# The expert stage of a decoder kernel: gate and up products side by side, and hidden rows turned in their own step

## The reference, cut to what matters

```python
logits = SOFTCAP * jnp.tanh((x @ w_gate) / SOFTCAP)
probs = jax.nn.softmax(logits, axis=-1)
_, idx = jax.lax.top_k(probs, TOPK)
weights = probs * jax.nn.one_hot(idx, E, dtype=probs.dtype).sum(-2)
for e in range(E):
    h = jax.nn.silu(x @ w1[e]) * (x @ w3[e])
    out = out + h @ w2[e] * weights[:, e:e + 1]
```

## Time and profile before

| | |
|---|---|
| time, median of 3 runs | 765.69 us (765.66 to 766.63) |
| profiled execution, its own time | 770.09 us |
| its span, first to last instruction | 767.6 us |
| granted TensorE clock, mean | 0.942 |
| busy in the span: PE, PEld, DVE, ACT, POOL | 654.6, 531.9, 483.6, 436.3, 201.2 us |
| expert stage, first gate product to the last result | about 614 to 742 us |

### The profile page before, as it was taken

The page is one execution under the profiler, slowest core; times in us unless marked ns, Lnnn a source line. Parts: engine busy times, 40 slices in busy tenths (PEclk is TensorE's granted clock), DMA queues, the critical chain, the costliest instruction groups (busy, mean ns, idle before and its releaser), DMA issues.

```text
span 767.6 us, 13772 instructions
## 1 busy us (share of the span) xinstructions
PE 654.6 (85%) x4748; PEld 531.9 (69%) x4749; DVE 483.6 (63%) x1091; ACT 436.3 (57%) x1123; POOL 201.2 (26%) x364
## 2 busy tenths in 40 slices
PE   6788787998999998878978999999986299999950
PEld 4566577998988988843545677777776178778840
DVE  1577776577586577475845656566557567777735
ACT  3988846457456456446866646464523256566622
POOL 2455510040010010011213334252326402223224
PEclk9999999999999999987999999999999589999985
DMA  8995000220220220043020000000078211111114
GB/s 303 378 321 165 1 1 1 86 87 1 88 86 1 86 87 1 1 194 81 1 83 1 1 1 3 1 1 2 1 304 327 68 30 48 48 55 48 48 46 145
DMA packets 31921, 62.02 MB, mean 81 GB/s; under 512 B 2452, under 2 KB 26776, under 8 KB 29624
## 3 DMA queue, kind: packets, MB, share of 16 engines
q1 hardware_dynamic: 29848, 56.04, 21.7%
q0 software_dynamic: 2016, 5.22, 1.9%
HBM read 45.80 MB, written 15.55 MB: 80 GB/s over the span
## 4 chain that ended last, share of the span: by engine, by line
PE 57%; ACT 19%; DVE 15%; issue 4%; POOL 3%; DMA 2%; SPq 0%; POOLq 0%; ACTq 0%; DVEq 0%
PE banks L1726 34%; PE bank L1726 23%; ACT arena L742 5%; DVE U_split L1205 4%; ACT arena L1010 4%; ACT U_split L761 2%; DVE mx L1159 1%; DVE dmx L1487 1%; ACT arena L1017 1%; POOL rstd L550 1%; POOL xs L646 1%; DMA ys<-arena 1%; ACT arena L780 1%; DVE arena L1444 1%; DVE bmx L1224 1%
## 5 line engine op out<-in xcount | busy, mean ns | idle before, releaser
L1726 PE MATMUL banks<-U_split 128*128 128x512 f32 (+1 forms) x616 | 147.8, 352 | 4.7 <-DVE U_split L1205 1.9
L1726 PE MATMUL bank<-U_split 128*128 128x256 f32 (+1 forms) x864 | 115.6, 290 | 15.3 <-DVE U_split L1205 15.2
L1726 PEld LDWEIGHTS bank<-U_split 128*128 128x128 f32 x864 | 108.6, 194 | 19.6 <-issue 15.0
L1726 PEld LDWEIGHTS banks<-U_split 128*128 128x128 f32 x616 | 97.0, 190 | 26.6 <-issue 11.6
L761 ACT ACTIVATE U_split<-arena 128x1024 fp32r (+6 forms) x122 | 97.2, 821 | 14.0 <-issue 5.3
L1726 PE MATMUL banks<-cst,arena 128*128 128x128 f32 (+1 forms) x594 | 83.7, 277 | 14.0 <-DMA arena<-xs 11.1
L1726 PE MATMUL banks<-arena 128*128 (+4 forms) x632 | 84.8, 382 | 8.3 <-ACT arena L1010 5.0
L547 POOL TENSOR_SCALAR rstd<-mv 128x1 f32<-128x1 f32 x48 | 11.8, 245 | 301.4 <-DVE mv L1137 269.5
L1726 PEld LDWEIGHTS banks<-cst,arena 128*128 128x128 f32 (+1 forms) x594 | 68.7, 142 | 24.0 <-issue 13.6
L1010 ACT ACTIVATE arena<-banks,dmx 128x128 f32<-128x128 f32 (+1 forms) x128 | 52.1, 419 | 53.8 <-DVE dmx L1487 53.8
L623 POOL TENSOR_SCALAR arena<-arena,dri 128x128 f32<-128x128 f32 (+1 forms) x128 | 52.6, 429 | 91.9 <-DVE dri L1455 91.9
(11 more groups left out here) (225 smaller groups left out, 1161.6 us busy)
## 6 DMA issues: line engine op xcount, KB each, us to landing
arena<-in_w_exp SPq DMA_DIRECT2D x8, 1536.0 KB, 14.3
xs<-arena SPq DMA_DIRECT2D x8, 1032.0 KB, 14.1
arena<-in_ctxT SPq DMA_DIRECT2D x4, 1601.0 KB, 7.2
arena<-in_ctx SPq DMA_DIRECT2D x4, 1536.0 KB
arena<-in_w_f SPq DMA_DIRECT2D x3, 1024.0 KB, 11.6
arena<-xs SPq DMA_DIRECT2D x23, 129.0 KB, 2.0
w_x<-in_w_x SPq DMA_DIRECT2D x9, 256.0 KB, 7.3
arena<-in_w_oh SPq DMA_DIRECT2D x1, 2048.0 KB, 8.1
```

Of the source, the lines that this page charges most:

```text
L1726: return nc.tensor.matmul(o, w, x, start=start, stop=stop, **k)
```

## The change

PE's order in step i becomes gate(i), up(i), tokens(i+1), down(i-1), hiddenT(i): the hidden rows of a tile are turned in its own step and no longer behind the next gate product. ACT reads the expert number and splits the gate weights of i+1 before silu(i). DVE's order becomes gate weights of i+1 (low), hidden(i), tokens of i+1 (low), up weights of i+1 (low), hiddenT copy(i). No instruction is added or taken away, and no buffer changes.

```diff
@@ ACT m_step
                 act.wait_ge(G["m_g"], i + 1)
                 if not first:
                     act.wait_ge(G["m_h"], i)
-                a.activation(sa, PS[0][:, :], ACT.Silu).then_inc(G["m_silu"], 1)
                 if not last:
                     e = expert(i + 1)
                     m_weights(e, 0)
+                a.activation(sa, PS[0][:, :], ACT.Silu).then_inc(G["m_silu"], 1)
+                if not last:
                     m_tokens(i + 1, 1 - slot)
                     act.wait_ge(G["m_u"], i + 1)
                     m_weights(e, 1)
@@ DVE m_step
-            def m_step(i, slot, first=False):
+            def m_step(i, slot):
                 e = expert(i + 1)
-                if not first:
-                    m_hiddenT(i - 1)
                 m_weights(i + 1, e, 0)
+                m_hidden(i)
                 m_tokens(i + 1, 1 - slot)
-                m_hidden(i)
                 m_weights(i + 1, e, 1)
+                m_hiddenT(i)
...
-            m_step(0, 0, first=True)
+            m_step(0, 0)
...
             m_step(TILES - 2, 1)
-            m_hiddenT(TILES - 2)
             m_hidden(TILES - 1)
             m_hiddenT(TILES - 1)
@@ PE m_step
                 m_half(i, 0, slot, "m_g")
-                if not first:
-                    m_hiddenT(i - 1)
+                m_half(i, 1, slot, "m_u")
                 if not last:
                     m_tokens(1 - slot, (h + (2 if slot else 1)) * 16)
-                m_half(i, 1, slot, "m_u")
                 if not first:
                     m_down(i - 1, expert(i - 1), free)
+                m_hiddenT(i)
...
             m_step(TILES - 1, TILES // 2, 0, last=True)
-            m_hiddenT(TILES - 1)
             m_down(TILES - 1, expert(TILES - 1))
```

## The result

The changed kernel takes 781.86 us (median of 4 runs, 780.62 to 783.34) against 765.74 before: a ratio of 1.0201, 95% interval 1.0178 to 1.0224. It is slower, 1.4 us beyond the predicted 780.5 and inside the range of 775.5 to 786.5. The profiled execution took 783.34 us with a span of 781.5.

The account below looks back on a forecast made before the run. PE was taken to bound the expert stage, busy 116.84 of 117.10 us, with each new wait paid in full. 13.0 + 1.3 - 0.44 + 1.0 = 14.9 on the median 765.69 gave 780.5 us, range 775.5 to 786.5.

Parts of the forecast that it names:

- 21 steps without the branch: Expert stage, gate product to gate product: each step 5.94 us in place of 5.32, 13.0 us in all.
- branch and queue on PE: PE's queue: branch and address arithmetic may show behind a wait ending a loop round; taken as 1.0 us, at most 3.2.
- first step: Tile 0 to tile 1: function table load moves behind the high part, next gate product at 622.45, not 621.16; 1.3 us.
- last step: Tile 22: tile 21's four transposes no longer stand between gate and up, so the closing copy comes 0.44 us earlier.
- the loop from gate product to gate product: Every step: gate product, register read, high part, low part, hidden, transposes, next gate product; links sum to 5.93, taken as 5.94.
- two ways to this last point: Next gate's weight load, reached over DVE's low part of the tokens at 5.93 or PE's three transposes at 5.91 us.
- One sign: Profile after: PE idle 0.6 to 0.8 us ahead of the four transposes, released by DVE's hidden product.
- PE's own work of a step: PE's demand for each tile: 12 matmuls 2.78, six transposes 0.66, down product 1.73, together 5.17 us.
- The claim about ACT: ACT in the loop: register read sets the split's start, so moving the silu behind it gains 0.
- The read did not vanish: Rival, ACT: register read costs nothing once silu is moved, high part 0.71 earlier, loop 5.23 us, total 764.0; 3%.
- PE's queue did not pay 0.36 each time: Rival, PE: work queued behind the transposes is decoded after the wait, 0.36 us on each of 21 steps, 787; 10%.
- The clock stayed at 1.00: Rival, PE: clock falls to 1.2 GHz in every fourth tile, 22 us more, 802; 3%.

Follow-up runs that it names:

- the experiment on the loop: Against the changed kernel, PE's hardware loop written out as a plain loop, other engines keeping theirs: 779.88 us, ratio 1.0159 to the kernel before.
- the best version here: The kernel before, with ACT reading the expert number ahead of the wait for the gate product: 766.52 us, ratio 0.9984; second set 765.79 us, ratio 0.9947.

## Why the prediction was right

Point by point, with what the trace shows for the terms of the sum:

| term | predicted | measured |
|---|---|---|
| 21 steps without the branch | +13.0 | +11.9 |
| branch and queue on PE | +1.0 | +1.6 |
| first step | +1.3 | +1.31 |
| last step | -0.44 | -0.44 |
| sum | +14.9 | +14.4 |

The steps together cost 125.32 - 111.76 = 13.56, of which the experiment on the loop takes out 1.64. The first two terms were off by 1.1 and 0.6 in opposite directions, so that the sum came out closer than its parts. The first step is 7.74 in place of 6.43 (613.62 to 621.36, before 614.73 to 621.16). From the gate product to the last down product of tile 22 it is 6.10 in place of 6.54 (746.68 to 752.78, before 732.92 to 739.46).

The part that carried the prediction, the loop from gate product to gate product, held link by link. Gate's weight load to low part was put at 3.65, measured 654.61 - 651.01 = 3.60, in the next step 3.68. Low part to hidden 1.15, measured 1.14. Hidden to the tokens' low part 0.59, measured 0.60. From there to the gate's weight load 0.54, measured 657.06 - 656.35 = 0.71 where the branch comes and 0.55 in the step before. The prediction had two ways to this last point, over the tokens' low part (5.93) and over PE's transposes (5.91). In steps without the branch they end together here too, 0.13 behind the low part and 0.41 behind the transposes' first weight load, so the trace does not say which one binds; with the branch it is PE's.

One sign was too high: PE was to idle 0.6 to 0.8 us ahead of the transposes. In the steps shown it idled 0.48 and 0.55 by its matmuls, 0.88 and 0.95 by its weight path, and 0.5 on average over the stage by the table of waits. The 5.17 us that the prediction took for PE's own work of a step is also at least 0.08 too much, as the steps of 5.09 show. The sum did not rest on it.

The claim about ACT, that the silu sits in the shadow of the register read, is shown three ways: by undoing ACT's order (nothing), by taking the read out (-0.60 a step), and by doubling it (+0.66). The table load moved behind the first high part as expected:

```profile
617.22 1.06 ACT L761 ACTIVATE U_split<-arena 128x1024 fp32r x1 [4.12 <-PE banks L1725]
...
618.30 1.28 ACT L1084 ACT_TABLE_LOAD   x1
...
619.59 0.60 ACT L1084 ACTIVATE arena<-banks 128x512 f32<-128x512 f32 x1
```

These rows are of the changed kernel. The silu starts 0.01 us after the load ends and the load 0.02 after the high part, so no drain shows between them. The Trainium skill, "ScalarE: Activation LUTs", section "What ACT_TABLE_LOAD costs", adds a drain of about 1.38 us to the load for every switch to a different set; this trace does not agree, and the measurement decides. The sum was right to leave it out, and that the time came out 1.4 us above the forecast has nothing to do with it, since the first step took what was forecast without a drain.

The rivals fell. The read did not vanish with the silu gone: the queue took 0.70 us from the end of the gate product. PE's queue did not pay 0.36 each time but 0.18 in 9 steps. The clock stayed at 1.00 with PE busy 114.79 of 125.30 us, as the rows of before had suggested.

Two of my later sizes were off. I priced ACT instructions end to end; back to back they overlap by 0.11, which is why the version with the read hoisted and the silu first was 0.11 a step better than expected. The same section of the Trainium skill says that back-to-back activations overlap by about 93 ns, and the trace agrees with its 0.10 to 0.11 us. And I took the register read as a constant of 0.28 us, where it took up to 0.54 beside SP's.

What stays open: the stage explains 14.4 us, the spans differ by 13.9, the profiled executions by 13.25, the medians by 16.1. The profiled execution of before lay 4.4 over its median, that of after 1.5 over its own. The stage itself starts 1.1 us earlier in the profile after (613.62 for 614.73), and what follows its last down product is 0.6 us longer, which together make 14.4 into 13.9. The remaining 1.7 us between stage and medians is in no row. It is less than the median of the kernel before moved between sets of runs (765.7 to 769.0).

What is left of the alternation between steps, 0.08 us, is ACT's. In every other step of its loop ACT's queue has a piece more ahead of the register read, for the wait on `m_h` (L1080):

```profile
658.76 0.04 ACTq L1080
...
659.54 1.07 ACT U_split L761
```

There the high part starts 659.54 - 657.06 = 2.48 after the gate's weight load, in the steps without that piece 2.40. With PE's loop written out the two are 2.47 and 2.41 still. That ACT's own loop branch is behind it was not tested.

## What to carry to other kernels

Before moving work ahead of an instruction, look at what really set its start. Here the chain of waits ran through a register read in ACT's queue and not through the silu, and moving that one read ahead of the wait gave back 0.60 of the 0.65 us that reordering three engines had cost a step. That does not make the new order as good as the old: with the same read moved in both, the old order takes 5.17 us a step and the new one 5.37. When a product on PE is to be consumed in the same step, count the whole way out through ACT and DVE and back: the work of the next tile that lies on it (here 1.06 us of high part and 1.14 us of low part) joins the loop. PE, busy nearly all the time, had only its holes to give, 0.15 us a step in the best version here, and what came in front of it was paid on each of the 21 steps.

## What the runs showed of the hardware that I had not expected

- The branch of PE's loop showed only behind a wait. With the transposes that wait for the hidden product at the end of a round it took 0.58 us from the transposes' to the next gate's weight load, in place of 0.39 with the loop written out. In the kernel before, where the down product ends a round, PE was busy 116.84 of 117.10 us with the same branch.
- A register read from on-chip memory by ACT's queue took 0.28 us when it ran alone and 0.32 to 0.54 when SP's queue read a register at the same time. That the one causes the other is not tested.
- An ACT instruction that follows another starts 0.10 to 0.11 us before the first one ends (654.37 against 653.41 + 1.06; 664.88 against 664.39 + 0.60).
